# The second image's conv inputs one slot later in a slotted schedule of eight image pairs

## The reference, cut to what matters

```
x = L0(x)   # per image: channel attention softmax(max(E) - E) with E = q q^T, out = attention @ q;
            # se = gate from the means of x and out;  se * x + (1 - se) * out
x = L1(x)   # reduce to 64 channels, depthwise 3x3, batch norm, relu; attention over the 2-D Fourier
            # features, a gated filter, a projection, + x
x = L2(x)   # group norm, 8-head self-attention over the 256 pixels of an image, a projection, + x
x = L3(x)   # q, k, v = conv3x3(x, Wq / Wk / Wv); attention between the 16 images at each pixel;
            # layer norm, relu, conv3x3(., Wc), + x
```

## Time and profile before

| | us |
|---|---|
| median of three runs | 499.03 (496.84 to 500.08) |
| the profiled execution, its time | 500.01 |
| the profiled execution, its span | 498.2 |
| mean granted PE clock in it | 0.974 |
| busy: PE / DVE / ACT / POOL | 465.4 / 344.7 / 249.3 / 126.4 |

### The profile page before, as it was taken

The page is one execution under the profiler, slowest core; times in us unless marked ns, Lnnn a source line. Parts: engine busy times, 40 slices in busy tenths (PEclk is TensorE's granted clock), DMA queues, the critical chain, the costliest instruction groups (busy, mean ns, idle before and its releaser), DMA issues.

```text
span 498.2 us, 10552 instructions
## 1 busy us (share of the span) xinstructions
PE 465.4 (93%) x3790; PEld 374.0 (75%) x3790; DVE 344.7 (69%) x890; ACT 249.3 (50%) x590; POOL 126.4 (25%) x154
## 2 busy tenths in 40 slices
PE   7999999988998999899899989999996999998896
PEld 6877765767586778677776867777774789898895
DVE  1448578867687787788777876876476442776895
ACT  3424756645555555555556455534633431294551
POOL 6022443474012112201120121120110011332762
PEclk9999999898899999999999999999997999998998
DMA  7100012030001001000100000000000000005112
GB/s 271 45 22 2 1 49 91 1 91 23 0 6 44 18 0 42 21 0 0 42 21 0 12 9 0 2 23 1 0 1 22 1 22 2 1 1 168 44 50 77
DMA packets 10639, 15.28 MB, mean 31 GB/s; under 512 B 624, under 2 KB 8944, under 8 KB 10480
## 3 DMA queue, kind: packets, MB, share of 16 engines
q1 hardware_dynamic: 10608, 14.86, 9.3%
HBM read 10.66 MB, written 4.19 MB: 30 GB/s over the span
## 4 chain that ended last, share of the span: by engine, by line
PE 71%; DVE 13%; ACT 6%; issue 4%; POOL 3%; DMA 1%; DVEq 0%; SPq 0%; ACTq 0%; POOLq 0%
PE bank L1232 10%; PE bank L1233 8%; PE bank L1234 8%; PE bank L1345 5%; PE bank L1437 5%; PE bank L1374 5%; PE bank L1411 3%; PE bank L1239 3%; PE bank L1409 2%; PE bank L1465 2%; PE bank L1452 2%; PE bank L1249 2%; DVE nmax L1007 1%; PE bank L1261 1%; PE bank L1297 1%
## 5 line engine op out<-in xcount | busy, mean ns | idle before, releaser
L1232 PE MATMUL bank<-win,w_hi 128*128 128x256 f32 x384 | 117.2, 305 | 2.6 <-POOL win L592 1.2
L1233 PE MATMUL bank<-win,w_hi 128*128 128x256 f32 x384 | 108.9, 284 | 0.0
L1234 PE MATMUL bank<-win,w_lo 128*128 128x256 f32 x384 | 108.7, 283 | 0.0
L751 ACT ACTIVATE prob<-bank 128x512 f32<-128x512 f32 x128 | 69.5, 596 | 69.7 <-PE bank L1409 69.0
L1007 DVE TENSOR_REDUCE nmax<-bank 128x2 f32<-128x512 f32 x128 | 84.9, 687 | 18.8 <-PE bank L1374 18.4
L1232 PEld LDWEIGHTS bank<-win,w_hi 128*128 128x128 f32 x384 | 73.1, 190 | 9.5 <-issue 1.6
L1233 PEld LDWEIGHTS bank<-win,w_hi 128*128 128x128 f32 x384 | 73.3, 191 | 0.4
L1234 PEld LDWEIGHTS bank<-win,w_lo 128*128 128x128 f32 x384 | 73.1, 190 | 0.0
L540 POOL TENSOR_TENSOR first<-first 128x256 f32<-128x256 f32 x24 | 17.7, 737 | 152.7 <-ACT first L643 152.7
L1239 PE MATMUL bank<-ones_r 128*128 128x256 f32 x276 | 50.0, 319 | 1.1 <-DVE ones_r L856 1.1
L1374 PE MATMUL bank<-qk 32*128 32x256 f32 x256 | 33.0, 335 | 12.7 <-DVE nmax L1007 7.2
(11 more groups left out here) (240 smaller groups left out, 900.0 us busy)
## 6 DMA issues: line engine op xcount, KB each, us to landing
w_stage<-convs SPq DMA_DIRECT2D x4, 576.0 KB, 4.0
x_t<-x_px SPq DMA_DIRECT2D x8, 256.0 KB, 3.1
x_in<-x SPq DMA_DIRECT2D x8, 256.0 KB, 2.8
out<-x_pair SPq DMA_DIRECT2D x8, 256.0 KB, 2.2
q<-out SPq DMA_DIRECT2D x1, 2048.0 KB, 8.4
out<-v SPq DMA_DIRECT2D x8, 256.0 KB, 2.1
cst<-small SPq DMA_DIRECT2D x1, 1712.0 KB, 9.1
cst<-small SPq DMA_DIRECT2D x1, 253.5 KB, 3.5
```

Source lines behind the costliest of these rows:

```text
L751: act.activation(prob[:, x // 4 % 2, x % 4, :, :], bank[ST_BANK[x % 2]][:, :], ACT.Exp, scale=L2_SCALE).then_inc(st_exp, 1)
L1232: mm(dst, hi, x_hi, start=(row == 0), stop=False)
L1233: mm(dst, hi, x_lo, start=False, stop=False)
L1234: return mm(dst, lo, x_hi, start=False, stop=(row == KH - 1))
```

## The change

Four numbers of tables move:

```diff
-POOL_SLOTS = {"rn": 1, "squares": 8, "diff0": 12, "grstd": 18}
+POOL_SLOTS = {"rn": 1, "squares": 8, "diff0": 14, "grstd": 18}
...
-WINDOW_SLOTS, ADD_SLOT, RESIDUAL_SLOT, HIGH_SLOTS, LOW_SLOTS = (3, 10), 6, 7, (8, 11), (11, 12)
+WINDOW_SLOTS, ADD_SLOT, RESIDUAL_SLOT, HIGH_SLOTS, LOW_SLOTS = (3, 11), 6, 7, (8, 12), (11, 13)
```

## The result

The changed kernel took 501.89 us (median of 11 runs, 501.16 to 505.79); the kernel before, run beside it, 498.97 us (11 runs, 496.84 to 500.19). The ratio is 1.0083, interval 1.0055 to 1.0112: slower by 0.8%, 2.9 us between the medians. The profiled execution of after was its longest: 505.79 us with a span of 504.0.

What follows compares the result with a forecast made beforehand. The prediction took PE's own work plus its waits as the bound; 0.7 (pair 1) + 2.1 (loop) + 0.4 (pair 6) - 0.6 (pair 7) = +2.6 us on 499.03 gave 501.6 us, range 498.2 to 504.8.

Steps and rivals of the forecast that it cites:

- the two terms of the loop: Gain in slot 12 and loss in slot 13: each of four trips 0.53 us longer, 2.1 us together.
- The gain in slot 12: Loop: maxima of slot 11 take the mixing's place on DVE, so PE goes on 0.71 us earlier, at 201.98.
- The loss in slot 13: Loop: PE's convolution waits about 1.3 us for image 1's later window_low, released at 206.19; trip 0.53 us longer.
- The upper bound of 0.79: Loop, slot 13: trip 0.79 us longer if POOL's difference needs its whole 1.81 us from its earlier start.
- Pair 1: Image 1's window_low falls on POOL's weight sum L499; +0.7 us, near the held end of 1.0 longer.
- Pair 6: No difference on POOL here, so the end without POOL is nearest: +0.4 us (0 to 0.5).
- Pair 7: Neither stages nor difference; PE's convolution begins at 383.26 in place of 383.89: -0.6 us (-1.0 to -0.3).
- Pair 0: Difference now behind the weight sums, done near 72, its reader x1 at 72.50: nothing, by half a us.
- The sum: Whole kernel: pair 1, loop, pair 6 and pair 7 together +2.6 us (0.0 to 4.4).
- A: Rival: window_low is done when filt ends, PE keeps its gains: -4.4 us, 494.6; chance 0.05.
- B: Rival: the slot-13 wait is as long as that of slot 12: 498.0 to 500.0 us; chance 0.13.
- C: Rival: a half-clock stretch in each of four trips, 4 x 1.7 on top: 508.4; chance 0.12, with a larger hold.

Runs made afterwards that it cites:

- e4_diff16: The change with GpSimd's difference in slot 16 in place of 14; 501.51 us (one run).
- e6_diff12: The change without its part on GpSimd, the difference staying in slot 12; 501.38 us (12 runs), ratio to before 1.0043.
- after again: The changed kernel, unchanged, for a second profile and more times; 502.91 us (12 runs), ratio to before 1.0070.
- before again: The kernel before, unchanged, for a second profile; 499.44 us (one run).
- e5_diff14_only: The kernel before with only GpSimd's difference moved, to slot 14 from 12; 499.02 us (12 runs), ratio to before 1.0013.
- the second set: The later timing of the unchanged changed kernel, 12 runs; 502.91 us, ratio to before 1.0070.
- e1_low12: The change with image 1's window_low in slot 12 in place of 13; 493.72 us (6 runs), ratio to before 0.9896.
- e9_low12_diff12: e1_low12 with GpSimd's difference back in slot 12 in place of 14; 493.68 us (6 runs), ratio to before 0.9900.
- e11_low12_again: e1_low12 unchanged, for more times; 494.5 us (7 runs), ratio to before 0.9911.
- e10_fill17: The change with six more filling matmuls of PE in slot 17 of pair 0 (12 in place of 6); 501.58 us (12 runs), ratio to before 1.0048.
- e12_diff12_again: e6_diff12 unchanged, for more times; 501.67 us (12 runs), ratio to before 1.0044.

## Why the prediction was right

The forecast was 501.6, the median 501.9: the two terms of the loop, which are most of the sum, came out as forecast, and so did the path that they take. Step by step:

**The gain in slot 12.** Predicted: PE goes on at 201.98, which is 206.10 on the time of after. Measured 206.14. The wait for a row maximum is gone, and on PE's line none for the exponentials is listed in its place. By the rows 0.09 us are left, as had been thought possible: PE's last matmul before ended at 206.05, the exponentials at 205.87.

**The loss in slot 13.** The difference was to begin beside image 0's `window_low` and to end 1.14 us after it, at 204.38: it ran from 206.95 to 208.50, which is 204.38. `att1_n` was to end 0.08 later, and ended 0.09 later, after 0.52 us. Then `window_low` to 210.26 and PE at 210.31, which is the 206.19 predicted. The wait shown is 0.93, not the 1.3 of the text: the profile counts it from the end of the last matmul of `filt` (208.79 + 0.60 = 209.39), and the 1.3 counts from where the next matmul could have begun, which before was 0.25 after the start of L1314. In the trip that makes no difference: 46.12 less 45.60 (the means) is 0.52, where the text has 0.53. The upper bound of 0.79, a difference that takes its full 1.81, did not come: the row maxima beside it took 0.68 and it was held only by the `window_low` ahead. This agrees with what the prediction took from the Trainium skill ("SBUF — State Buffer", "Who interferes with whom"): a tensor_reduce went on unhindered, 0.68 and 0.69 us with and without POOL, and of two that contend the second waited. The 1.14 us, read from one row of before, came again: the difference takes 1.28 us where it begins first (e4_diff16), and in both kernels it ended 1.14 behind the `window_low` that had begun before it.

**Pair 1.** The step was +0.7, with L499 holding `window_low`. In the trace of after:

```profile
113.67 0.99 POOL L499 TENSOR_TENSOR v<-v,w_stage 128x384 f32<-128x384 f32 x1
...
114.14 1.08 DVE L1036 TENSOR_TENSOR win<-windows,win 128x512 fp32r<-128x512 f32 x1
...
115.27 0.38 PE L1232 MATMUL bank<-win,w_hi 128*128 128x256 f32 x1 [0.90 <-DVE win L1036]
```

It is held, 1.08 in place of 0.68. Between profiles with one half-clock stretch of 3.4 us in pair 1, the pair alone took 50.93, 50.97 and 51.04 us with the change's windows (e6_diff12 and again, after again) and 50.35 and 50.38 without (before again, e5_diff14_only): +0.6 to +0.7. The size is in part luck: 0.7 was a choice between two ends, 1.0 and -0.55, and no sum.

**Pair 6.** +0.4 was predicted; the table gives +0.1 and +0.3, and +0.4 in e6_diff12 (43.84).

**Pair 7.** −0.6 was predicted. Between the two profiles with the same 6.8 us at half clock there, before again and after again, it is 132.14 − 132.59 = −0.45. Its wait of 2.17 us became one of 1.17 for exponentials. In e6_diff12 and again, where the half clock lasted 10.2 us there and 6.8 in place of 3.4 near 453, this piece took 133.70 and 133.57, a microsecond more than before; in after, with 10.2 us there alone, it was −0.1. So the gain is there and the clock may take it back.

**Pair 0.** "Nothing, by a margin of half a us" holds for the waits and not for the clock. The reader of the difference, x1, indeed does not wait for POOL, and the pair takes no longer where the clock stays at 1.00 (43.53 to 43.77 us with the two new waits, 43.43 to 43.69 without). What the step left out is that, with the difference no longer ahead of them, PE and DVE come earlier to what follows, and `z0p` falls beside L499; and that the clock can fall there, which cost about 1.3 and 2.8 us in the two profiles of after. Whether the one brings the other is the open point above.

**The sum.** +2.6 was predicted. Its measured terms, 2.1 + 0.6 to 0.7 + 0.1 to 0.4 − 0.45, make 2.35 to 2.75; the medians differ by 2.9 in the first set, and by 4.2 in the second; without POOL's part by 2.7 and 3.0. That the median came within 0.3 us of the forecast is partly luck: the clock in pair 0 was no term of it, and the second set's median is 502.9.

**The rivals.** A (the gain stays) and B (one wait for another) are excluded by the trip, about 0.5 us longer in all four. e1_low12 shows where A's condition holds: one place earlier for `window_low`, and DVE is in time. C, the clock, did not come in the loop: the windows of after over the last three of its four trips give

```profile
189.50:327.90 138.40, 132.79 (x1131) 100.94 (x1130) 104.67 (x281) 74.89 (x183) 22.20 (x30) 1.00 0.05 13
```

with the wait of a microsecond in each. It did come in pair 0, where the prediction did not look for it. What it took from the Trainium skill ("TensorE: Matmul & The Clock Gate", "What's actually happening"), that the monitor runs free of the kernel, fits the table, in which the same kernel has more or fewer such stretches: before itself has 10.2 us of half clock in pairs 0 and 1 in one profile and 3.4 in the other.

## What to carry to other kernels

A step taken out from ahead of one release must be followed to its new place on the same engine: here 0.7 us were gained at one wait and 1.2 lost at the next, and the same mixing with only its last operation one slot earlier made the kernel 1.0% faster than before. To find the length of a wait that will arise, write the late engine's program as a list with the durations of the trace, and take for operations that contend with another engine the end of the one that holds them, not their own length. When an operation is moved, look also at what the others in its engine's program then come to lie beside.

## What was not expected of the hardware

Even a tiny operation is held to the end of the other: `z0p`, 128 x 2 numbers, took 0.70 and 0.73 us beside POOL's L499 in the two profiles of after, ended 0.02 us behind it in both, and takes 0.16 where it begins behind L499 (e9_low12_diff12). The 128 x 128 `att1_n` took 1.10 us in before, 0.52 in after and 0.29 in e4_diff16, where POOL was idle beside it.

Two waits of PE of 0.25 to 0.28 and 0.60 to 0.61 us, with 0.6 us of work between them, were followed by half clock in both profiles of after. The same two in four profiles of three other kernels were not (0.41 and 0.60 in e11_low12_again), nor a single one of 0.42 (e10_fill17), 0.46 (e6_diff12) or 0.60 (e12_diff12_again). In the loop 0.71 and 0.93 us, 5 us apart, left the clock at 1.00 in every trip. What decides it no run here settles.
